# Moving the sign add of a guarded residual from VectorE to GpSimd in a fused LoRA and cross-attention kernel

## The reference

```python
# layer 0: a LoRA mixture with a router, lora_A = ctx (4 x 64 x 1024)
w = softmax(x @ router_W.T + router_b)            # 8 weights per token
a_sum = einsum('bsh,arh->bsr', x, lora_A)         # 64 per token
y = einsum('bsr,nhr->bsnh', a_sum, lora_B)
out = x + 0.5 * einsum('bsn,bsnh->bsh', w, y)
x = nan_to_num(out, nan=0.0, posinf=10000.0, neginf=-10000.0)
# layer 1: cross-attention to 64 context rows, 32 heads of 32, then a LayerNorm
Q, K, V = x @ Wq.T + bq, ctx @ Wk.T + bk, ctx @ Wv.T + bv
attn = softmax(where(mask, Q K^T / sqrt(32), -inf))
x = x + (attn V) @ Wo.T + bo
x = (x - mean) / sqrt(var + 1e-5) * ln_g + ln_b
```

## Time and profile before

| what | us |
|---|---|
| median of three runs | 723.1 |
| the profiled execution | 723.1 |
| its span | 721.3 |
| TensorE busy | 678.7 |
| VectorE busy | 498.0 |
| ScalarE busy | 294.7 |
| GpSimd busy | 209.3 |

### The profile page before, as it was taken

How to read it: one execution, slowest core, us unless ns; L and a number is a source line. 1 busy time by engine, 2 the same in 40 slices (tenths; PEclk the granted TensorE clock), 3 DMA queues, 4 the chain that set the end, 5 groups by cost and what they waited for, 6 DMA issues and landing times.

```text
span 721.3 us, 10742 instructions
## 1 busy us (share of the span) xinstructions
PE 678.7 (94%) x3622; PEld 580.2 (80%) x3622; DVE 498.0 (69%) x946; ACT 294.7 (41%) x891; POOL 209.3 (29%) x217
## 2 busy tenths in 40 slices
PE   8999969899898998999968999999999999999993
PEld 6888758688786887778857888888888888888882
DVE  5789863477535775457745568888888888888644
ACT  4532231211213111311205566666666666666511
POOL 0200000200010000200212234366666666666644
PEclk9999979999999999999989999999999999999997
DMA  8965574223566237651345699352435254523311
GB/s 309 308 220 162 184 231 112 117 74 87 204 239 243 76 97 265 205 204 44 117 122 109 236 372 361 86 151 84 156 108 151 85 161 119 161 88 103 117 59 58
DMA packets 100886, 115.18 MB, mean 160 GB/s; under 512 B 41312, under 2 KB 75232, under 8 KB 100832
## 3 DMA queue, kind: packets, MB, share of 16 engines
q1 hardware_dynamic: 100832, 114.50, 49.1%
HBM read 68.33 MB, written 46.14 MB: 159 GB/s over the span
## 4 chain that ended last, share of the span: by engine, by line
PE 76%; issue 14%; DVE 7%; ACT 1%; DMA 1%; POOL 0%; DVEq 0%; SPq 0%; ACTq 0%; POOLq 0%
PE ps L518 23%; PE ps L520 22%; PE ps L519 22%; PE ps L660 4%; PE ps L569 3%; DVE q_sb L829 2%; PE ps L601 1%; DMA stage<-WkT 1%; PE ps L581 1%; DVE h_t L819 1%; DVE h_t L816 1%; DVE x_sb L803 1%; DVE hn_sb L792 1%; DVE u_lo L781 1%; ACT q_sb L997 0%
## 5 line engine op out<-in xcount | busy, mean ns | idle before, releaser
L518 PE MATMUL ps<-act_hi,w_hi 128*128 128x512 f32 x256 | 106.8, 417 | 14.2 <-DVE q_sb L829 10.8
L518 PE MATMUL ps<-wo_hi,cx_hi 128*128 128x512 f32 x256 | 104.5, 408 | 0.0
L520 PE MATMUL ps<-act_hi,w_lo 128*128 128x512 f32 x256 | 104.3, 407 | 0.0
L1019 ACT ACTIVATE s_sb<-s_sb,s_min 128x64 f32<-128x64 f32 x256 | 86.3, 338 | 43.5 <-DVE s_min L855 43.5
L519 PE MATMUL ps<-act_lo,w_hi 128*128 128x512 f32 x256 | 104.0, 406 | 0.0
L1080 POOL TENSOR_TENSOR u_sb<-a_sb,w_sb 128x512 f32<-128x512 f32 x16 | 20.0, 1274 | 281.7 <-DVE w_sb L775 267.4
L520 PE MATMUL ps<-wo_hi,cx_lo 128*128 128x512 f32 x256 | 100.3, 392 | 0.0
L519 PE MATMUL ps<-wo_lo,cx_hi 128*128 128x512 f32 x256 | 100.2, 391 | 0.0
L991 ACT ACTIVATE act_hi<-h_t 128x512 fp32r<-128x512 f32 x32 | 20.2, 632 | 181.3 <-DVE h_t L819 181.3
L1098 POOL TENSOR_TENSOR s_sb<-s_sb,s_min 128x256 f32<-128x256 f32 x64 | 39.3, 614 | 151.2 <-DVE s_min L855 151.2
L850 DVE SCALAR_TENSOR_TENSOR s_sb<-ps,mask_f 128x512 f32<-128x512 f32 x64 | 44.2, 691 | 54.4 <-PE ps L520 52.8
(11 more groups left out here) (110 smaller groups left out, 1526.9 us busy)
## 6 DMA issues: line engine op xcount, KB each, us to landing
q_cols<-q_sb SPq DMA_DIRECT2D x32, 512.0 KB, 4.4
qb<-q_cols SPq DMA_DIRECT2D x64, 256.0 KB, 3.5
x_sb<-xT SPq DMA_DIRECT2D x32, 256.0 KB, 3.0
h_rows<-hn_sb SPq DMA_DIRECT2D x32, 256.0 KB, 3.1
output_weights<-wo_sb SPq DMA_DIRECT2D x32, 256.0 KB, 2.6
z_sb<-h_rows SPq DMA_DIRECT2D x16, 512.0 KB, 4.6
out<-z_sb SPq DMA_DIRECT2D x16, 512.0 KB, 2.9
stage<-WkT SPq DMA_DIRECT2D x8, 512.0 KB, 7.5
```

The costliest lines, as they stand in the source:

```text
L518: pe.matmul(dst, lh, rh, start=(first and j == 0), stop=False)
L520: mm = pe.matmul(dst, ll, rh, start=False, stop=(last and j == n - 1))
L1019: act.activation(s_sb[c % 4][:, h, :], s_sb[c % 4][:, h, :], ACT.Exp, bias=s_min[c % 2][:, h:h + 1], scale=-1.0, accum_out=s_sum[c % 2][:, ...
```

## The change

The add of pos and neg leaves VectorE's `select`. GpSimd gets a stage `update` of its own, which it runs for each of the 32 columns at the place of `update` in the list. It waits for both sign ops of its column, for the transposes of column m - 3, which read the same buffer of h_t, and for act_lo of that column. The predicated copy stays on VectorE, behind the waits for finite and for the add. GpSimd's queue is now expand, then the adds of a batch in order, and `zero` behind the add of column 31.

```diff
             def select(i, c):
                 m = KC * i + c
-                dve.wait_ge(sign_step, 2 * m + 2)
-                wait(dve, hn_mm, m - 2)
-                wait(dve, hhi_done, m - 2)
-                dve.tensor_tensor(h_t[m % 3][:], pos[m % 2][:], neg[m % 2][:], ALU.add).then_inc(sign_ready, 1)
                 dve.wait_ge(f_ready, m + 1)
                 dve.wait_ge(sign_ready, m + 1)
                 dve.copy_predicated(h_t[m % 3][:], finite[m % 2][:], x_sb[:, c, :]).then_inc(h_ready, 1)
...
+            def signs(m):
+                pool.wait_ge(sign_step, 2 * m + 2)
+                wait(pool, hn_mm, m - 2)
+                wait(pool, hlo_done, m - 2)
+                pool.tensor_tensor(h_t[m % 3][:], pos[m % 2][:], neg[m % 2][:], ALU.add).then_inc(sign_ready, 1)
+
+            def update(i, c):
+                signs(KC * i + c)
+
             def zero():
                 pool.wait_ge(up_mm, ALL)
...
-            run({"expand": expand, "zero": zero, "step": step})
+            run({"expand": expand, "update": update, "zero": zero, "step": step})
```

## The result

The changed kernel took 729.38 us, the median of five runs (727.64 to 730.46), against 723.05 for the kernel before in runs beside it. The ratio is 1.0091, 95% interval 1.0070 to 1.0111: 6.3 to 6.6 us slower. The forecast was 3.25 us. The change went the forecast way and the time lies 0.12 us inside the stated range, but the forecast size is only half of what came.

A forecast was written before the change was run, and what follows sets the result against it. TensorE, busy 678.7 of 721.3 us, was taken as the bound; 3.95 + 1.2 + 1.2 - 2.25 - 0.85 = + 3.25 us on 723.1 gave 726.3 us, range 722.7 to 729.5.

The forecast's parts named there:

- three kinds of place: Batch 0, VectorE nearly without rest; middle columns of batches 1 to 3, 1.05 us slack; batch ends, one chain delaying TensorE.
- rival 2: Longer stands ending batches 1 and 2 draw slow clock stretches, no batch 3 gain: 728.7 or 730.2 us; chance 0.17.
- Batch 0: Columns 0 to 6: add waits behind the split, 7 x 0.55 - 0.5 slack = 3.35 us late at column 6's copy.
- Column 7: Last column of batch 0, no split between, on the same chain: + 0.6 us.
- The hand-overs: VectorE to GpSimd and back: copy starts 0.6 us later per column where nothing stands between.
- price of 1.29 for the add: GpSimd's add taken at 1.29 us, with 1.04 as lower bound; it took 0.68 on VectorE.
- End of batch 3: Columns 6 and 7 add 1.2 us, finite of column 31 no longer shut out gives - 3.45: - 2.25 us.
- Its part by the memsets: End of batch 3: memsets come after finite of column 31 instead of shutting it out, - 3.45 us.
- The queues and the later memsets: Later memsets delay neither VectorE nor loads into zeroed tiles; expand() and x loads find their queues in time: no cost.
- Rivals 1 and 3: 1: batch 0 add runs beside split, 723.0 us, 0.20 with cheap add; 3: memsets block predicated copy, 733.4, 0.06.
- TensorE's clock: Shorter batch 3 stand gives back 1.45 us, longer stands at batches 1 and 2 cost 0.6: net - 0.85.
- ends of batches 1 and 2: Columns 6 and 7 of each batch lie on the chain, 2 x 0.6 each: + 1.2 and + 1.2 us.

## Why the prediction was half right

*The bound and the three kinds of place* held. Middle columns cost nothing alone (721.68 against 721.79). That the time lies inside the range is luck: 729.38 against a bound of 729.5, a bound that was set to take in half of rival 2.

*Batch 0* was forecast as + 3.35 at the copy of column 6: measured 3.42 in the trace, and +3.4 in the run that has this part alone. The add ends 1.11 behind the split, for 1.15 forecast; the rule of the Trainium skill (SBUF — State Buffer, Who interferes with whom), taken to the letter (1.29), is too much by 0.18, and the trace's earlier meeting was the better guide. Column 7 gave 0.45 for 0.6. TensorE's waits for kv_sb and hn_sb from 80 to 150 us grew from 6.1 to 9.8 us, for "over 3 us" foretold.

*The hand-overs* cost 0.63 per column, for 0.6 forecast, and the price of 1.29 for the add was right (1.28 to 1.29).

*End of batch 3*: 14.79 us from x_sb of column 6 to the copy of column 7 became 12.63, - 2.16 for - 2.25 forecast. Its part by the memsets, - 3.45, measured -3.6 alone. Undone, with the one add back on VectorE, it cost 3.2, for 2.8.

*The queues and the later memsets*: no cost of theirs shows. The loads that TensorE waits for behind batch 3, once it gets there earlier, are those of the queries, and the forecast didn't have this wait (2.8 us with the memsets alone held back, 0.4 in the changed kernel). Rivals 1 and 3 are out: no add ran beside a split, and the copy took 0.73 inside a memset.

*TensorE's clock* is the step that failed: "I put that at 0.6 and take - 0.85 net". The mechanism was named and its size at batches 1 and 2 was wrong. Without it the steps sum to + 4.1, and the trace has 3.42 + 0.45 + 1.29 + 1.28 - 2.16 = + 4.3. Behind batch 3 the shorter stand did halve the slow stretch and give back: from the last copy to the end 356.0 us became 355.0 and 355.1, about - 1.0 for - 1.45 forecast. The mistake was at batches 1 and 2. I took 3.3 us (measured: 3.0) to be "nearer to 2.35 than to 5.8" and so gave the growth of the stands 0.6. But a stand of 2.35 mostly draws no slow stretch (2 in 9), while one of 3.0 draws one each time (12 in 12). So the pieces behind it go from 39.1 to 40.7 nearly always, 2 x 1.6, less what the kernel before has of this itself: + 2.5 by the stands (12 in 12 against 2 in 9), + 2.1 by the pieces (9 in 10 against 2 in 8). Net about + 1.1 to + 1.5, in place of - 0.85. The run with these ends alone has 5.8 - 2.5 = 3.3 for it, with an interval of 1.3 to either side. That was rival 2's mechanism, at a chance of 0.17, though not its whole condition: it had no gain behind batch 3.

The error in reading is plain afterwards. The earlier trace rows show one slow stretch behind a stand of 2.35 us, at batch 1. The same trace has a second stand of this length, at batch 2, with no slow stretch behind it (the piece of 39.07 above). One look at it would have shown that 2.35 lies where it goes either way, and that 0.65 us more can't be taken as nearly nothing.

4.3 + 1.5 are 5.8 of the 6.3 to 6.6 (5.4 with the lower figure). The rest isn't assigned. A candidate is batch 0: between 88 and 146 us the four profiles with column 7's add on GpSimd have four or five slow stretches, and the eight others three each. What that costs isn't shown, for from the copy of column 6 to the first x_sb of batch 1 the four take 56.6 to 58.3 us and the others 56.4 to 57.6. Pieces of the time vary from execution to execution (from the copy of column 7 of batch 0 to the next x_sb: 43.0 us before, 44.4 and 43.0 in the two profiles of the changed kernel), and the intervals are 1.4 us to either side.

The parts timed alone are consistent with this: batch 0 3.4, ends of batches 1 and 2 5.8, middle 0, memsets - 3.6, and by the trace 0.45 for column 7 and 2 x 0.63 for batch 3, sum + 7.3, each part with an interval of 1 us or more.

## What to carry to other kernels

An op moved to an idle engine pays only where its old engine was the bound; here 18 of 32 adds were free, and the others stood on chains, where a hand-over and a slower engine cost 0.45 to 0.65 us each. Price a longer stand of TensorE twice, once for its length and once for what the clock does behind it, and look at all stands of like length in the trace before setting that second price. And look at what else the moved work reorders in its new queue: the only gain of this change came from memsets that happened to be pushed out of the way, and one wait had it alone.

## What the runs showed of the hardware

A GpSimd memset shuts out VectorE's finite, an op with one input and one output in SBUF, but not a copy or subtraction with two SBUF inputs (0.73 and 0.68 inside a memset). GpSimd's add is shut out by such a subtraction (2.17 for 1.29). The Trainium skill (SBUF — State Buffer, Who interferes with whom) says that a VectorE instruction with two SBUF inputs contends with a GpSimd instruction that reads SBUF and not with one that only writes it, and that one in a mode that uses both port pairs, which a tensor_scalar such as finite can enter, contends with any; the trace agrees.

The section speaks of one instruction blocking another. How long a row of four memsets keeps finite out isn't fixed. In four profiles it got in only when the last was done (issued at 359.94 while the second still ran, to 360.04, and through at 363.82, just behind the last at 363.53; 3.23 to 3.88 us for 0.43). In three others it got in behind the third memset, and then pos was shut out by the fourth:

```profile
356.83 2.13 DVE L807 TENSOR_SCALAR finite<-x_sb 128x512 uint8<-128x512 f32 x1
358.88 2.10 DVE L808 TENSOR_SCALAR pos<-x_sb 128x512 f32<-128x512 f32 x1
```

These two are of the kernel before with the row copy first. Either way neg starts 7.5 to 7.6 us behind the start of the first memset.

TensorE's clock falls to 1.2 GHz behind some stands of 2.3 us and behind all of 3.0 and more, of the 36 for the row copy in the table above. 0.65 us of waiting was worth up to 2.2, its length and 1.6 for the clock.
